# Node update of a graph network: one group after another, against bodies that span three groups

## What is computed

```python
x1 = attention over the 8 heads of each node
attn_out = segment_sum(x1[dst] * x1[src], dst)
h = _layernorm(x + attn_out @ O_w + O_b, ln1_w, ln1_b)
ffn = relu(h @ f1_w + f1_b) @ f2_w + f2_b
h = _layernorm(h + ffn, ln2_w, ln2_b)
gi, gh = h @ gru_w_ih + gru_b_ih, h @ gru_w_hh + gru_b_hh
r, z = sigmoid(gi_r + gh_r), sigmoid(gi_z + gh_z)
n = tanh(gi_n + r * gh_n)
x_mid = _layernorm(x + (1 - z) * n + z * h)
table = x_mid @ [W, W a_s, W a_t]      # what the second layer gathers
```

## Time and profile before

| what | value |
|---|---|
| median of three runs | 2984.2 us (2983.03 to 2986.73) |
| profiled execution, its time | 2989.73 us |
| its span, first to last instruction | 2988.0 us |
| mean granted TensorE clock | 0.963 of full speed |
| node update, from the first L754 to the last L809 | 1406.95 to 2043.09 us |
| busy share of the span: TensorE, VectorE, ScalarE, GpSimd | 90%, 79%, 45%, 18% |

### The profile page before, as it was taken

One profiled execution on the slowest core, in us unless ns is written; L12 is line 12 of the kernel. 1 busy time (PEld: TensorE's weight loads), 2 busy tenths in 40 slices (PEclk: granted clock), 3 DMA queues, 4 the chain that ended last, 5 costly groups with the idle time before them and its releaser, 6 DMA issues. The chain is left out here.

```text
span 2988.0 us, 48177 instructions
## 1 busy us (share of the span) xinstructions
PE 2689.0 (90%) x15118; PEld 2018.4 (68%) x15118; DVE 2368.3 (79%) x4217; ACT 1354.2 (45%) x2825; POOL 547.0 (18%) x547
## 2 busy tenths in 40 slices
PE   2699979999999999996888787886999999999996
PEld 1366646666666666664555455554999999999996
DVE  5699978888888888884666565666998989898896
ACT  0123347777777777773323232334543333333332
POOL 5489950000000000000122221120000000000000
PEclk6799999999999999998999999997999999999998
DMA  1111102221222212224011211014555464554543
GB/s 49 47 45 44 40 36 94 93 91 72 93 93 93 93 72 90 93 93 145 24 60 62 63 62 59 3 37 115 131 106 120 87 116 88 110 120 82 120 88 72
DMA packets 405300, 239.23 MB, mean 80 GB/s; under 512 B 325488, under 2 KB 397040, under 8 KB 398864
## 3 DMA queue, kind: packets, MB, share of 16 engines
q1 hardware_dynamic: 383968, 215.53, 26.4%
q10 hardware_dynamic: 19824, 19.32, 2.0%
q0 software_dynamic: 1344, 2.41, 0.3%
HBM read 47.69 MB, written 110.84 MB: 53 GB/s over the span
## 5 line engine op out<-in xcount | busy, mean ns | idle before, releaser
L1375 PE MATMUL b_pagg<-x_parts,b_counts 128*128 128x512 f32 x2401 | 790.4, 439 | 0.0
L1755 PE MATMUL d_acc<-d_rows_high,d_weights_high 128*128 128x258 f32 x2401 | 685.8, 286 | 19.5 <-DVE d_weights_low L1621 11.7
L1756 PE MATMUL d_acc<-d_rows_low,d_weights_high 128*128 128x258 f32 x2401 | 679.4, 283 | 0.0
L1757 PE MATMUL d_acc<-d_rows_high,d_weights_low 128*128 128x258 f32 x2401 | 678.6, 283 | 0.0
L1335 DVE TENSOR_TENSOR b_key_hot<-b_keys,b_ends 128x1176 bf16<-128x1176 f16 x784 | 601.5, 767 | 0.0
L1695 ACT CAST d_weights_high<-d_weights 128x896 fp32r<-128x896 f32 x343 | 322.3, 945 | 536.2 <-PE d_acc L1757 274.2
L1390 PE MATMUL b_pcounts<-b_key_hot,b_lo_hot 128*128 128x392 bf16 x2352 | 526.4, 334 | 13.2 <-DVE b_key_hot L1335 12.5
L1420 ACT CAST b_counts<-b_pcounts 128x392 fp32r<-128x392 f32 x784 | 381.6, 487 | 259.2 <-PE b_pcounts L1390 257.4
L1375 PEld LDWEIGHTS b_pagg<-x_parts,b_counts 128*128 128x128 f32 x2401 | 435.4, 189 | 91.0 <-ACT b_counts L1421 0.7
L1755 PEld LDWEIGHTS d_acc<-d_rows_high,d_weights_high 128*128 128x128 f32 x2401 | 455.7, 190 | 28.4 <-DVE d_weights_low L1621 15.3
L1756 PEld LDWEIGHTS d_acc<-d_rows_low,d_weights_high 128*128 128x128 f32 x2401 | 455.8, 190 | 2.2 <-issue 2.2
(11 more groups left out here) (161 smaller groups left out, 2768.5 us busy)
## 6 DMA issues: line engine op xcount, KB each, us to landing
edge_counts<-b_counts SPq DMA_DIRECT2D x49, 1568.0 KB, 5.1
node_table<-u_table ACTq DMA_DIRECT2D x7, 903.0 KB, 9.3
qx<-in_x SPq DMA_DIRECT2D x49, 128.0 KB, 2.1
x_table<-x_tile ACTq DMA_DIRECT2D x49, 128.0 KB, 1.7
agg<-b_sums SPq DMA_DIRECT2D x49, 128.0 KB, 4.6
u_x<-x_table SPq DMA_DIRECT2D x7, 896.0 KB, 8.9
u_agg<-agg SPq DMA_DIRECT2D x7, 896.0 KB, 11.3
u_x<-in_x SPq DMA_DIRECT2D x7, 896.0 KB, 4.9
```

The source lines that it names most:

```text
L1375: last = nc.tensor.matmul(pagg[:, o, :], ca[:, o, hi, :], x1_parts[:, hi].rearrange("p m d -> p (m d)"), start=(hi == 0), stop=(hi == TILE ...
L1755: nc.tensor.matmul(acc[:, r, 0:HT], a, high[:, t, :], start=(t == 0), stop=False)
L1756: nc.tensor.matmul(acc[:, r, 0:HT], a, low[:, t, :], start=False, stop=False)
L1757: last = nc.tensor.matmul(acc[:, r, 0:HT], b, high[:, t, :], start=False, stop=(t == TILES - 1))
```

## The change

All engines now follow one table. An item is (kind, number, group offset), and one body of the steady program, `BODY`, holds work of three groups: the second half of group b (offset 0: f1, f2, h2, gates), the end of group b-1 (offset -1: last tanh and mix, gru, xmid, table), and the beginning of group b+1 (offset 1: times, attn, O, h1). A gate quarter is split into four items "gate" of one `half_matmul` each, and VectorE's and ScalarE's parts of a quarter are the items "new" (L788, L791 before), "tanh" and "mix" (`combine`). The program is a start ("head"), a body for group 0 ("first"), two passes of a loop with two steady bodies, one steady body outside of it, and "last" and "tail".

```diff
-UPDATE_STEPS = (
-    ("attn", 0), ("attn", 1), ("O", 0), ("attn", 2), ("O", 1), ("attn", 3), ("O", 2), ("attn", 4), ("O", 3), ("attn", 5),
...
+BODY = (("f1", 0, 0), ("tanh", 3, -1), ("gru", 0, -1), ("f1", 1, 0), ("mix", 3, -1), ("gru", 1, -1), ("f1", 2, 0), ("gru", 2, -1),
...
+        ("gate", 4, 0), ("tanh", 0, 0), ("attn", 2, 1), ("O", 1, 1), ("gate", 5, 0), ("mix", 0, 0), ("attn", 3, 1), ("O", 2, 1),
...
+def update_bodies(eng, run):
+    run(Body("head", -1, 1, 0, 0))
+    run(Body("first", 0, 0, 2 * GROUP, GROUP))
+    with eng.Fori(0, (GROUPS - 3) // 2) as i:
+        for k in range(2):
+            b = 2 * i + 1 + k
+            run(Body("steady", b, (1 + k) % 2, b * TP, b * MO))
+    run(Body("steady", GROUPS - 2, (GROUPS - 2) % 2, (GROUPS - 2) * TP, (GROUPS - 2) * MO))
+    run(Body("last", GROUPS - 1, (GROUPS - 1) % 2, (GROUPS - 1) * TP, (GROUPS - 1) * MO))
+    run(Body("tail", GROUPS, GROUPS % 2, (GROUPS - 1) * TP + 3 * GROUP, (GROUPS - 1) * MO + 2 * GROUP))
```

```diff
-        for j, name in enumerate(("O_b", "ln1_w", "ln1_b", "f2_b", "ln2_w", "ln2_b")):
+        for j, name in enumerate(("O_b", "ln1_w", "ln1_b", "f2_b")):
             sp.dma_start(self.rows[:, j, :], self.w[name].partition_broadcast(P)).then_inc(self.first_in, 16)
+        for j, name in enumerate(("f2_b", "ln2_w", "ln2_b")):
+                sp.dma_start(self.cols[:, j, :], self.w[name].rearrange("(m p) -> p m", p=P)).then_inc(self.first_in, 16)
...
+                def evacuate_columns(B, s, dst, scale, bias):
+                    act.wait_ge(tp_full, B.tp_full(s))
+                    for k in range(KC):
+                        last = nc.scalar.activation(dst[:, k, :], tp[:, B.tp_bank(s), tile(k)], ACT.Identity,
+                                                    scale=scale[:, k:k + 1] if scale is not None else 1.0, bias=bias[:, k:k + 1])
+                    last.then_inc(tp_out, 1)
```

The transposes back ("gru") now go into the banks `mo`, from which VectorE adds x at once, so that ScalarE's copy for them is gone; the "table" matmuls go into the banks `tp`. x has two buffers, h1 and h2 have transposed buffers of their own, and the product of x1 and agg is written in place. SyncE loads the next group's x1 when the transposes of the last body are done:

```diff
+                    wait_over_zero(sp, tp_full, B.turned0)
+                    load(at[:], x1, g, x1_in)
+                    if B.kind != "head":
+                        sp.wait_ge(attn_ready, GROUP * g)
+                    load(agt[:], agg, g, agg_in)
+                    if B.kind == "steady":
+                        sp.wait_ge(mo_out, B.mo_full(("gru", GROUP - 1, -1)))
+                    load(xt[:, (B.odd + 1) % 2], x, g, x_in)
```

VectorE finishes a row of "O", "f2" or "gru" (`SUMMED`; the last operation of its norm, `finish`) behind the statistics of the next row, or at an item "norm":

```diff
+                        elif what in SUMMED:
+                            dve.wait_ge(mo_full, B.mo_full(s))
...
+                                stats_of(B, s, h[:, n, :])
...
+                            for older in waiting:
+                                finish(B, older)
+                            waiting = [s]
```

More of the change, by code:

```diff
@@ new lines @@
+END = (("tanh", 3, -1), ("gru", 0, -1), ("mix", 3, -1), ("gru", 1, -1), ("gru", 2, -1), ("xmid", 0, -1), ("gru", 3, -1), ("xmid", 1, -1),
+       ("table", 0, -1), ("gru", 4, -1), ("xmid", 2, -1), ("table", 1, -1), ("gru", 5, -1), ("xmid", 3, -1), ("table", 2, -1),
+       ("gru", 6, -1), ("xmid", 4, -1), ("table", 3, -1), ("norm", 0, -1), ("xmid", 5, -1), ("table", 4, -1), ("xmid", 6, -1),
+       ("table", 5, -1), ("table", 6, -1))
+PLANS = {"head": START, "first": tuple(s for s in BODY if s[2] >= 0), "steady": BODY,
+         "last": tuple(s for s in BODY if s[2] <= 0), "tail": END}
@@ L497, in _, with load @@
             def _(sp):
[L498 to L506, removed]
+                def load(dst, src, g, sem):
+                    sp.dma_start(dst, src[group_rows(g), 0:D].rearrange("(n p) d -> p n d", p=P)).then_inc(sem, 16)
@@ new lines, in body @@
+                def body(B):
+                    if not any(s[2] == 1 for s in PLANS[B.kind]):
+                        return
+                    g = B.group(1)
+                    wait_over_zero(sp, tp_full, B.turned0)
[6 more added lines that the diff above has]
+                    load(xt[:, (B.odd + 1) % 2], x, g, x_in)
+                    if B.kind == "head":
@@ L541, in step @@
                         if n < 2:
[L542 to L561 removed]
+                            wait_over_zero(pe, gates, GAT * g)
+                        elif n < 4:
+                            wait_over_zero(pe, new_pre, GQ * g)
+                        else:
+                            pe.wait_ge(relued, REL * g + n - 3)
@@ L594, in group @@
-                def group(g):
-                    for what, n in UPDATE_STEPS:
-                        step(g, what, n)
-                group_steps(pe, group)
+                        turn(B, s, xm[:, n, :])
+                    elif what == "table":
+                        pe.wait_ge(tp_out, B.tp_full(("xmid", n, dg)))
+                        pe.wait_ge(tp_out, B.tp_free(s))
+                        for k in range(KC):
+                            last = nc.tensor.matmul(tp[:, B.tp_bank(s), 0:HT], tT[:, k, tile(n)], weights.w1[:, k, :],
+                                                    start=(k == 0), stop=(k == KC - 1))
+                        last.then_inc(tp_full, 1)
@@ L599, in _, with body @@
+                def body(B):
+                    for s in PLANS[B.kind]:
+                        step(B, s)
+                update_bodies(pe, body)
                 pe.wait_ge(tp_out, TP * GROUPS)
@@ L665, in _, with body @@
+                def body(B):
+                    for s in PLANS[B.kind]:
+                        step(B, s)
+                update_bodies(act, body)
                 act.wait_ge(stored[0], 16 * GROUPS)
```

454 lines of the change are left out of this document (255 added, 199 removed), and 3 rows, old and new, of the table UPDATE_STEPS.

## The result

The changed kernel takes **2875.9 us** (median of 4 runs, 2873.8 to 2879.1) where the kernel before took 2985.5 beside it: a ratio of **0.9634**, 95% interval 0.9617 to 0.965. Run again on the chip of three of the experiments (`after_again`), it gave 0.9648, 0.9632 to 0.9665. The forecast was 2886, with a range of 2862 to 2916. Whole times differ by some 6 us from chip to chip with the stage as long as before (first f1 to last instruction 507.2 and 507.8 us), so experiments are compared by ratio and by stretches of the trace.

What follows compares the result with a forecast made beforehand. TensorE, 68.5 us of work per 88.5 us group, loses time to waits on VectorE. Steady bodies of 71.6 us plus 1 of slip, with head, end bodies, tail and branch, give a 538 us stage, 98 less: 2886 us, range 2862 to 2916.

Steps and rivals of the forecast that it cites:

- TensorE's work: Steady body: the same matmuls stay, 68.5 us on TensorE, which sets the pace; VectorE has 52.5 us.
- xmid 0: Start of stretch f1: TensorE reaches xmid 0 at 5.1 us, VectorE finishes its row at 6.8; 1.9 us wait with handoff.
- Start of f1: Between bodies: f1 0 waits for the copy of the last h1 row, now two ACTIVATEs; 1.2 us in all.
- Slip: Gates: balanced middle quarters make two just-missed waits per body, 1 us each body, 7 us over seven bodies.
- Branch: Loop's branch back: one instead of two in the stage, costing 6.5 us.
- Start: Head of the stage: one more load and three of single elements queued ahead of x1 on SyncE, 1 us.
- First body: Body of group 0, without the old group's gru, xmid and table and the wait at xmid: 60.5 us.
- Last body: Body of the last group, without the next group's attn, O and h1 rows: 62.4 us.
- The loads: x1 and agg loaded at body start land 11.3 us after issue, at no cost; rival of late landing +18 us, chance 0.08.
- VectorE paces the gates: Rival, middle gate quarters: GpSimd's additions slow VectorE, 1.7 us more per quarter, +30 us, 2916 us; chance 0.15.
- Lock-step: Rival, whole body: half of some 80 TensorE items met 0.54 us late, 21.6 us per body, 3009 us; chance 0.05.
- Straight-line program free, only the taken branch pays: Instruction fetch: the longer straight-line program costs nothing; only a taken branch outside the window waits, trace showing 6.84 us.

Runs made afterwards that it cites:

- e8_best: Changed kernel with loop written out, xmid and table one f1 item later, and f1's first half waiting only for its own four h1 rows: 2857.3 us, ratio 0.9549.
- e7_gate_vector: Changed kernel with two more VectorE operations of 128 x 448 per gate quarter, results thrown away: 2892.7 us, ratio 0.9686 to the kernel before.
- e2_gate_blocks: Changed kernel with the four gate items of each quarter together and the next group's rows behind them: 2961.6 us, ratio 0.9919 to the kernel before.
- e3_unrolled: Changed kernel with its loop of two passes of two bodies written out, no branch back in the stage: 2874.1 us, ratio 0.9606 to the kernel before.
- e10_gate_pairs: Changed kernel with gate items two and two, the next group's rows between the pairs: 2898.7 us, ratio 0.9709 to the kernel before.
- e4_xmid_later: Changed kernel with the rows of xmid and of the table one f1 item later: 2874.4 us, ratio 0.9601 to the kernel before.
- e5: Changed kernel with f1's first half waiting only for the copies of its own four h1 rows: 2877.4 us, ratio 0.9619 to the kernel before.
- e6: Changed kernel with two more VectorE operations of 128 x 256 per f2 row, results thrown away: 2895.0 us, ratio 0.9699 to the kernel before.

## Why the prediction was right, step by step

- *TensorE's work, 68.5 us per body, sets the pace*: right. `e8_best` has it bare: 68.25.
- *xmid 0, 1.9 us*: 1.62 idle. *Start of f1, 1.2*: 1.18 from transpose to matmul, the two ACTIVATEs 364 ns each. By the formula of the Trainium skill (ScalarE: Activation LUTs, "What ACT_TABLE_LOAD costs") the estimate was 1.3; the trace has the smaller one. The steady bodies without the branch took 71.5, 71.5, 71.4 and 70.7, against 71.6. That the sum is so near is in part luck: the two gaps are 2.4 us of idle time, not 3.1, but TensorE is busy for 69.0 us around them, not 68.25.
- *Slip, 1 us per body*: **this is the term that was mis-sized.** There is none; the starts in a middle quarter have no gap. It was put there because the quarter was balanced at 9.5 to 9.8 us, and `e7_gate_vector` shows more room than that: 4.1 us of added work cost 2.1. It makes 7 of the 10 us between the forecast for the stage (538) and 527.8.
- *Branch, 6.5*: 5.3, now on VectorE instead of ScalarE. *Start, 1 us*: 0.3 (14.85 us from the first load's issue to the first product, 14.52 before). *Head, 20.7*: 20.6. *First body, 60.5*: 62.0, its f1 ran at a granted clock of 0.88. *Last body, 62.4*: 60.9; that these two misses cancel is luck. *Tail, 21.8*: 22.4.
- *The loads, no cost*: right, and with room, 7.9 us where I took 11.3.
- *VectorE paces the gates* (0.15): did not happen, but the reason given against it held only in part. L873, the operation that L708 was, took 475 ns on average over all 49 rows, where a slow L708 took 1.03 us. GpSimd's additions slow other operations instead: once in each of six bodies an L842 of a mix takes 1.03 us in place of 0.62, and an L832 of an h2 row 0.81 in place of 0.41. Here is one, with the addition beside it; TensorE's starts in the middle quarter shown above have no gap in the same microseconds.

```profile
1608.61 1.03 DVE L842 TENSOR_TENSOR u_rT<-u_rT,u_zT 128x448 f32<-128x448 f32 x1
```

```profile
1608.02 1.13 POOL L791 TENSOR_TENSOR u_x_plus_bias<-u_x,rows 128x256 f32<-128x256 f32 x1
```

- *Lock-step* (0.05): did not happen either, but `e2_gate_blocks` shows that it exists. With other positions in the same table a body loses 15.7 us again, though the kernel stays 0.8% under the one before. The price that I gave it (21.6 us per body) was near only by luck: it was worked out from forty short waits of 0.54 us, and the trace has a few long ones, up to 2.9 us, and a lower clock behind them. What decides is how many items stand in a block, not a mean per item.
- *Straight-line program free, only the taken branch pays*: `e3_unrolled` has five bodies of 70.73 us without a branch, and no stall by issue. The Trainium skill (Runtime: NRT & Kernel Launch, "Instruction fetch mechanics") says that prefetch is sequential, and that a taken branch to a target outside the window has to wait for its fetch; `e3_unrolled` agrees. Two runs with the branch but without the stall (last section) don't fit it as plainly.
- Stated as a reason and not quite so: I spoke of lost time as idle time only. The kernel before also ran its groups at a lower clock than the one group of the earlier trace rows. Its windows, two groups that follow later:

```profile
1693.90:1782.70 88.80, 76.60 (x279) 49.38 (x279) 55.83 (x154) 27.59 (x63) 19.59 (x28) 0.94 0.16 52
1782.70:1878.10 95.40, 76.83 (x279) 49.11 (x279) 54.60 (x154) 27.51 (x63) 19.60 (x28) 0.93 0.16 49
```

The sum held because it set the whole stage of before against bodies at full clock. From the first f1 to the end, TensorE's idle time fell from 104.5 to 26.6 us and its busy time from 516.0 to 480.7, so 78 of the 113 us are idle time. Of the 35 us of busy time the clock has a part only: a group of before is busy for 75.5 us on average, the one at full clock for 73.1, and a body of the changed kernel for 69.0. So the clock gives some 2.4 us per group. The other 4 are there at full clock and go with the gaps: the same records are busy for 69.9 us in `e10_gate_pairs`, with 5.3 us of gaps, and for 68.3 in `e8_best`, with none.

## What to carry to other kernels

Read the matmul work from starts of records, add the waits whose chain can be named, and forecast that. Don't add a general allowance for handoffs where the slower engine has slack within each stretch: here there was no slip at all, or, with rows in blocks, 15.7 us of it. Place items so that the slow engine meets one row at a time, and give a stall on the side (a branch, a late copy) an item of the bound engine to hide behind. Price work taken off an engine, or a copy made longer, in the order in which it will run: here the copies cost 18 us of the stage in one order and show as 5 in the other, and the saved additions gave next to nothing and 19.

## What was unexpected of the hardware

- Stands of TensorE cost twice. Behind 3.98 us (changed kernel), 3.64 us (`e7_gate_vector`) and 2.87 us (`e2_gate_blocks`) the next records ran at the lower level for a while; behind 2.47 us (`e4_xmid_later`) and 1.62 us they did not. The length of the last stand alone does not decide it: in the kernel before, the records behind a stand of 3.29 us (at 1661.0) ran at a granted clock of 1.00, and those behind one of 1.88 us (at 1775.8) at 0.52.
- The stall behind the branch moves to whichever engine is short of work, and it is not always there. In the changed kernel VectorE's first addition of that body starts 4.31 us after the transpose that it needs, and in the other bodies of the loop 0.60. In `e10_gate_pairs` it is 0.98 and in `e2_gate_blocks` 0.60, and the body behind the branch is as long as the others to 0.5 us. Why the same loop stalls VectorE for 5.1 to 5.5 us in four kernels (the changed one, `e4`, `e5`, `e6`) and not in these stays open; no run was made for it. In `e7_gate_vector` the stall hides under another name: the profile puts the wait down to TensorE, but the addition starts 2.48 us after its transpose. These 1.9 us come out as TensorE's wait (3.64 us, 1.73 in the body before), and the other 3 of the 5 us go with the lower clock.
- Two ACTIVATEs of 128 x 128 with a bias took 0.36 us each, and with weight and bias 0.45 each, where one COPY of 128 x 256 took 0.37.
